# Third row score of an attention step moved behind the extra TensorE work

## The reference

```
xn = layernorm(x)
# differential attention, 16 heads, two maps of width 16 per head
Q, K, V = xn @ Wq, xn @ Wk, xn @ Wv
A1 = softmax(Q1 @ K1.T * scaling)
A2 = softmax(Q2 @ K2.T * scaling)
out = (A1 - lamb * A2) @ V            # per head, 1024 x 1024 maps
out = layernorm(out @ Wo) * gamma + beta
# feed-forward branch: q, k, v by a routed tree of 16 leaves each
q, k, v = fff(xn), fff(xn), fff(xn)
ffn = softmax(q @ k.T / sqrt(256)) @ v
result = x + out + ffn
```

## Time and profile before

| | |
|---|---|
| timed runs | 4268.96, 4272.05, 4272.66 us; median 4272.05 |
| span of the profiled execution | 4262.0 us |
| TensorE busy | 3874.9 us (91%) |
| VectorE busy | 3105.8 us (73%) |
| ScalarE busy | 2850.4 us (67%) |
| GpSimd busy | 1328.1 us (31%) |
| mean granted TensorE clock | 0.953 of full speed |

### The profile page before, as it was taken

One profiled execution on the slowest core, in us unless ns is written; L12 is line 12 of the kernel. 1 busy time (PEld: TensorE's weight loads), 2 busy tenths in 40 slices (PEclk: granted clock), 3 DMA queues, 4 the chain that ended last, 5 costly groups with the idle time before them and its releaser, 6 DMA issues. The chain is left out here.

```text
span 4262.0 us, 76116 instructions
## 1 busy us (share of the span) xinstructions
PE 3874.9 (91%) x23970; PEld 1577.6 (37%) x23970; DVE 3105.8 (73%) x5547; ACT 2850.4 (67%) x3429; POOL 1328.1 (31%) x1618
## 2 busy tenths in 40 slices
PE   3379999999999999999999999999999949979999
PEld 2123223323323233233223323322332215668888
DVE  3568897898788878987997888788889613434444
ACT  0017887888788878877887888788888946722221
POOL 4211421232134214221421233133214137763420
PEclk8669999999999999999999999999999979989999
DMA  9720111111111111111211111111111029842320
GB/s 317 251 65 24 51 58 42 41 56 40 48 36 56 46 36 47 62 54 32 65 36 51 36 53 39 47 41 59 55 36 58 24 106 359 276 125 90 99 80 20
DMA packets 224807, 332.04 MB, mean 78 GB/s; under 512 B 29297, under 2 KB 165236, under 8 KB 219780
## 3 DMA queue, kind: packets, MB, share of 16 engines
q1 hardware_dynamic: 205956, 276.47, 19.8%
q0 software_dynamic: 18432, 50.36, 3.6%
HBM read 169.34 MB, written 156.34 MB: 76 GB/s over the span
## 5 line engine op out<-in xcount | busy, mean ns | idle before, releaser
L1516 DVE TENSOR_REDUCE arena<-psum 128x1 f32<-128x512 f32 x4096 | 2597.0, 683 | 481.4 <-PE psum L1089 445.4
L1320 ACT ACTIVATE arena<-psum,arena 128x1024 f32<-128x1024 f32 x2048 | 2161.2, 1110 | 193.9 <-PE psum L1127 170.3
L1089 PE MATMUL psum<-arena 48*128 48x512 f16 x4096 | 1385.7, 395 | 80.4 <-DVE arena L1516 22.4
L1143 PE MATMUL psum<-arena 128*32 128x512 f32 x8200 | 1109.5, 613 | 1.4 <-ACT arena L1244 0.7
L1089 PEld LDWEIGHTS psum<-arena 48*128 48x128 f16 x4096 | 323.0, 93 | 1648.5 <-DVE arena L1516 1116.8
L1127 PE MATMUL psum<-arena 50*128 50x512 f16 x4096 | 877.8, 384 | 50.6 <-issue 28.1
L1382 POOL TENSOR_TENSOR arena<-arena 128x16 f32<-128x16 f32 x129 | 28.6, 222 | 1779.4 <-DVE arena L1526 1779.4
L1075 PE MATMUL psum<-arena 128*128 128x256 f32 x1024 | 291.2, 410 | 11.0 <-DVE arena L1516 11.0
L749 ACT ACTIVATE mix_arena<-psum,mix_arena 128x1024 f32<-128x1024 f32 x64 | 71.3, 1114 | 321.8 <-DVE mix_arena L769 321.8
L1252 ACT ACTIVATE arena<-psum,arena 128x256 f32<-128x256 f32 x256 | 121.2, 474 | 230.6 <-PE psum L1075 230.3
L1127 PEld LDWEIGHTS psum<-arena 50*128 50x128 f16 x4096 | 210.1, 94 | 167.7 <-ACT arena L1320 89.9
(11 more groups left out here) (165 smaller groups left out, 3040.5 us busy)
## 6 DMA issues: line engine op xcount, KB each, us to landing
arena<-scratch_split SPq DMA_DIRECT2D x768, 64.0 KB, 2.1
scratch_split<-arena SPq DMA_DIRECT2D x64, 512.0 KB, 3.2
scratch_sorted_x<-route_arena SPq DMA_DIRECT2D x60, 512.0 KB, 8.1
leaf_arena<-scratch_sorted_x SPq DMA_DIRECT2D x60, 512.0 KB, 6.0
scratch_sorted_y<-leaf_arena SPq DMA_DIRECT2D x60, 512.0 KB, 4.1
leaf_arena<-in_leafw SPq DMA_DIRECT2D x3, 5128.0 KB, 19.3
arena<-in_x SPq DMA_DIRECT2D x18, 512.0 KB, 4.3
scratch_sum<-arena SPq DMA_DIRECT2D x18, 512.0 KB, 3.0
```

What stands on the lines that cost most here:

```text
L1089: nc.tensor.matmul(aux_bank[bank], ring[at, slot, 0, m, qt * P:(qt + 1) * P], ring[at, slot, 1, m, c * CH:(c + 1) * CH], start=True, stop=True
L1143: last = nc.tensor.matmul(value_bank[32 * j:32 * j + 32, :], vaug[:, kt, 2 * (s % PER_BATCH) + j % 2, :], prob[:, step % 2, j, :], start=k ...
L1320: nc.scalar.activation(prob[:, step % 2, 2 * h:2 * h + 2, :], score[:, 2 * h:2 * h + 2, :], ACT.Exp, scale=exp_scale[:, s % 2, s // 2:s // ...
L1516: nc.vector.tensor_reduce(halfmax[:, odd, 2 * m + h, qt, c:c + 1], aux_bank[bank], AX.X, ALU.max).then_inc(bank_used[bank], 1)
```

## The change

`uses` puts the extra of a step between the second and the third row score in place of between the third and the fourth:

```
     def uses(s, step, tail):
 
         row = rows(s, step, tail)
-        return row[:3] + extras(s, step, tail) + row[3:]
+        return row[:2] + extras(s, step, tail) + row[2:]
```

## The result

The changed kernel takes 4322.5 us (median of 4 runs, 4320.5 to 4323.69) where the kernel before took 4270.5 us beside it (4 runs, 4266.13 to 4272.66): ratio 1.0123, 95% interval 1.0109 to 1.0138. It is slower by 52 us, clear of the 0.2% that can be told from no change. 4347 us was forecast (+75); the measured time lies within the range given.

A forecast was written before the change was run, and what follows sets the result against it. Steps with extra work were taken as TensorE's own work, plain steps as bound by VectorE's read of r2. +10.0 us per full iteration, seven times +70, plus +5.2 in the last, made +75: 4347 us, range 4315 to 4372.

The forecast's parts named there:

- v step: Step with a v projection as extra work, value block to value block: 3.55 us forecast, 3.35 before.
- r1 at T + 1.18: Of a step's row scores r0 to r3, r1 loads 1.18 us after T, r3's load, once VectorE has read r2.
- o steps: Steps whose extra work is of kind o: forecast +0.20 us each.
- Shift: Steps with a shift extra, where ScalarE's long read of the transposed shift already delays the banks: -0.11 us each.
- Turn: Four turn steps per full iteration, where a longer ScalarE read already delays r1 a little: +0.12 us each.
- Plain steps: Steps without extra work, bound by the loop through VectorE's read of r2: still 2.49 us.
- 0.52 us loss: Per changed step, r1 waits for the read of r2, so the value block comes at T + 1.49, not T + 0.97.
- 0.32 us gain: Per changed step, r2's old place ahead of the extra is saved, since beside r3 it costs nothing.
- three stalled steps: Three steps of every iteration, during a layer norm's statistics: -1.8 us together, between -0.6 and -3.
- Rival A: Faster: r1 finds its bank free, loading before about T + 0.97; full 0.32 us kept gives 4086 us; chance 0.05.
- Rival B: No change, 4272 us: stalled steps, iteration starts and shift steps give back at least 75 us more; chance 0.04.
- Rival C: Slower, 4427 us: the wait ahead of r1 recurs in all steps and TensorE's granted clock falls; chance 0.05.

The follow-up runs named there:

- read256_before: Kernel before the change, but VectorE's maximum reads only the first 256 of 512 columns of each row score: 4126.9 us, ratio 0.9672.
- read128_before: Kernel before the change, but VectorE's maximum reads only 128 of 512 columns of each row score: 4102.1 us, ratio 0.9610.
- read128_after: Changed kernel, but VectorE's maximum reads only 128 of 512 columns of each row score: 4043.9 us, ratio 0.9474 to the kernel before.

## Why the prediction was right, and where its sizes were off

**Direction and mechanism: right.** The v step was put at 1.00 + 1.06 + 1.18 + 0.31 = 3.55 us and is 3.55. r1 at T + 1.18, released by VectorE, is what the rows show. o steps: +0.20 forecast, +0.20 measured. Shift: -0.11 forecast, -0.13 measured. Turn: +0.12 and +0.10. Plain steps: none and none.

**The two halves of the term.** The 0.52 us loss is shown by the shorter reads: 0.27 us less read gave 0.27 us less step in the v steps (3.55 to 3.28) at an order otherwise the same. The 0.32 us gain can be read off the rows after the change: the extra follows the value block at once (1.00 us), and r2 loads with r3. The shorter read bears out both at once: 0.52 less 0.27 is a loss of 0.25, less the 0.32 it is -0.07, and the v steps became 0.07 us shorter than in the old order.

**The size: off by 23 us, around the stalls, at the iteration's start and in the qk steps.** Per full iteration +10.0 us was forecast; the traces show 7.2 on the mean (50.6 us over seven), and 4.6 in the last, where 5.2 was forecast. The terms that were mis-sized, per full iteration and on the mean:

- The three stalled steps gave 2.50 us back where I took 1.8 (-0.70).
- The first step of an iteration became 0.47 us shorter where I took +0.20 (-0.67). It runs at a low clock behind the loop's branch. In six iterations the granted clock was 0.50 to 0.52 before and 0.57 to 0.63 after, and the step became shorter, mostly 5.58 us in place of 6.22; in the first iteration it became 0.49 us longer.
- The steps (1,5), (1,6) and (2,5), (2,6), next to the statistics, became 0.57 us shorter together where I took +0.18 (-0.75).
- The other 29 qk steps cost 0.18 us each and not 0.20, since some of them lasted 3.41 before and all last 3.55 after (-0.70).
- The steps behind the second square root took 0.3 us more, where I took nothing.

Nearly all of these go the same way, so the total is not right by errors that cancel. The mechanism behind the first was not in the forecast. I wrote that TensorE's order is not what these steps wait for. The 1.67 us wait in (1,2) was for just that: for the bank of r0, which the order gives to the extra. I had only the later r1 hidden by the stall, not that the extra would pass the stalled read and take ScalarE's square root with it. That the clock would stay up there was not forecast either, and why it does is open, so this part of the size was not something that the rows could give.

**A sign that was named wrong.** I wrote that the idle time ahead of line 1089's loads, as ended by line 1516, would grow by 200 us and that TensorE's busy time would fall. The first fell from 1116.8 to 916.1 us. The second rose from 3874.9 to 3901.1, of which 11.1 us lie in the loop; why it rose was not looked into. Every load behind a value block carries 0.84 us of idle time and is put down to whoever released it last, although the array was busy with the block all the time. After the change that entry stands ahead of the extra in the changed steps (line 1081 in the rows above) and no longer ahead of line 1089. A wait that ends while the array is busy costs nothing, and the group's sum mixes both. VectorE's own idle time, +109 us, was the usable sign.

**Rival A (pairing gained, read not in the way): fell**, at the read's present length. Its break-even of r1 at T + 0.97 held: with r1 at T + 0.90 the new order is the faster one. The rule behind it, of the Trainium skill ("TensorEngine Tiling (Array Packing)", Tiling Modes), that tiles operate independently, agrees with the trace: r2 and r3 both load at 1555.63. It says what the array can do and nothing of who waits for the bank.

**Rival B (no change): fell**, though it named the right place. The stalled steps, the iteration's start and the shift steps had to give 9.4 us per iteration more than I took; with the steps next to the statistics they gave some 2.3 (0.70 + 0.67 + 0.75 + 0.14).

**Rival C (clock): fell.** The granted clock of the loop is 0.99 after and 0.98 before, with a wait of some 0.5 us ahead of r1 in nearly all of its steps. In the stalled steps it fell in six of the eight iterations before and in none after. The rule named with it, of the Trainium skill ("TensorE: Matmul & The Clock Gate", "A second HAM failure mode: psum-queue depth-cycling"), would have had the clock swing; no run here shows it for waits of this length.

## What to carry to other kernels

Where few buffers go round in turn, moving an instruction moves which reader the later ones wait for; write down for each use which read frees its buffer, and how long after issue that read is over, before counting the array's time. Put the uses with the slowest reader ahead of the work that can cover the read, and choose by the length of that work: 1.06 us covered two reads here, 0.59 us did not. A per-step price read from two kinds of steps of the old profile carried to 0.01 us. What did not carry were the few steps in which other work stalls, so count those apart and look at what the moved instruction lets past. Look also at the step behind a changed one: when an order makes a step shorter than the reader's own work in it, the wait turns up in the next. And look at each iteration before giving a cause to a median: here the clock fell in six of eight.

## What the runs showed of the hardware that was not expected

- The read of a 512-column fp32 bank by VectorE's reduction takes 683 ns, of 256 columns 417, of 128 columns 288 (profiles of `before`, `read256_before` and `read128_before`): by these some 0.13 us per 128 columns and 0.15 to 0.16 us fixed, an estimate.
- Whether the clock falls at a stall can differ from one iteration to the next: before, with the same pauses of 1.37, 0.86 and 0.40 us between TensorE's matmuls, the three stalled steps took 13.5 us at a granted clock of 1.00 in two iterations and 15.1 us at 0.89 in five.
- Half-array matmuls start closer to each other than their own length: in `read128_after` the loads of r0, the second score pair and r1, four matmuls, stand within 0.23 us (1422.56 to 1422.79), where one row score's matmul takes 0.39 us on the mean, and the value block of all 128 rows comes 0.62 us after the first of them.
